# Layer 0: each pair of value products as four products of 32 columns, in a kernel of four graph layers

## What is computed

```
h = relu(layernorm(x))
Q, K, V = h @ Qw + Qb, h @ Kw + Kb, h @ Vw + Vb
S1 = einsum('id,kdh->ikh', Q, A1);  S2 = einsum('jd,kdh->jkh', K, A2)
e = S1[rows[:, None], kidx] + S2[rows[None, :], kidx]       # kidx: the edge's kind, from adj
attn = softmax(leaky_relu(e), axis=1)
x = x + einsum('ijh,jhd->ihd', attn, Vh).reshape(n, h * d) @ Pw + Pb
```

## Time and profile before

| | |
|---|---|
| median of 3 runs | 1069.88 us (1066.89 to 1075.04) |
| the profiled execution, its own time | 1069.17 us |
| its span, first to last instruction | 1066.9 us |
| busy: PE, DVE, POOL, ACT | 941.1, 732.8, 554.4, 552.6 us |
| mean granted clock of TensorE | 0.893 |
| layer 0's loop over tiles | about 94 to 575 us of the span |

### The profile page before, as it was taken

How to read it: one execution, slowest core, us unless ns; L and a number is a source line. 1 busy time by engine, 2 the same in 40 slices (tenths; PEclk the granted TensorE clock), 3 DMA queues, 4 the chain that set the end, 5 groups by cost and what they waited for, 6 DMA issues and landing times.

```text
span 1066.9 us, 14476 instructions
## 1 busy us (share of the span) xinstructions
PE 941.1 (88%) x5214; PEld 331.4 (31%) x5214; DVE 732.8 (69%) x1181; ACT 552.6 (52%) x957; POOL 554.4 (52%) x658
## 2 busy tenths in 40 slices
PE   1998999999999999999999379899968949999970
PEld 1853222222222222222224322233332324555430
DVE  3234777777787777877774558611539577999987
ACT  0465666666566665666652047300120138899970
POOL 2005788888989888898781000000000007899962
PEclk8655999999999999999998569999968965999995
DMA  9472011121112112021000000000000000000000
GB/s 197 75 157 73 11 22 63 34 70 35 66 27 67 37 27 74 22 73 33 22 16 7 0 1 1 1 1 1 1 0 1 1 1 0 1 1 1 0 1 20
DMA packets 24764, 32.99 MB, mean 31 GB/s; under 512 B 16187, under 2 KB 16315, under 8 KB 23670
## 3 DMA queue, kind: packets, MB, share of 16 engines
q1 hardware_dynamic: 22390, 23.69, 7.8%
q0 software_dynamic: 2304, 8.39, 4.3%
HBM read 39.17 MB, written 1.29 MB: 38 GB/s over the span
## 4 chain that ended last, share of the span: by engine, by line
PE 74%; DVE 15%; issue 4%; ACT 3%; DMA 2%; POOL 1%; SPq 1%; DVEq 0%; POOLq 0%
PE ps L1102 22%; PE ps L1112 11%; PE ps L1239 8%; PE ps L1089 5%; DVE big L405 4%; PE ps L1081 4%; PE ps L1187 3%; PE ps L1264 3%; PE ps L1300 3%; PE ps L1032 2%; PE ps L993 2%; DVE big L734 2%; DMA big<-in_L_gnn_Pw_dram 2%; DVE big L402 2%; PE ps L1177 2%
## 5 line engine op out<-in xcount | busy, mean ns | idle before, releaser
L538 DVE COPY_PREDICATED big<-mask,ps 128x512 f32<-128x512 uint8 x512 | 338.4, 723 | 109.4 <-PE ps L1089 102.2
L362 POOL TENSOR_SCALAR big<-big 128x512 f32<-128x512 f32 x512 | 355.2, 710 | 67.2 <-PE ps L1112 66.7
L861 ACT ACTIVATE ps<-ps 128x512 f32<-128x512 f32 x512 | 266.8, 583 | 159.8 <-PE ps L1081 159.8
L1102 PE MATMUL ps<-big 128*64 128x512 f32 x1024 | 258.9, 613 | 0.0
L374 POOL TENSOR_TENSOR big<-big 128x512 f32<-128x512 f32 x40 | 67.3, 1682 | 328.7 <-ACT big L939 328.7
L1112 PE MATMUL ps<-big 128*32 128x512 f32 x1024 | 136.3, 604 | 0.0
L1081 PE MATMUL ps<-op_r,op_l 18*128 18x512 bf16 x512 | 109.7, 385 | 1.8 <-DVE mask L530 1.2
L1102 PEld LDWEIGHTS ps<-big 128*64 128x64 f32 x1024 | 58.6, 136 | 135.6 <-issue 98.7
L1300 PE MATMUL ps<-big 66*128 66x512 f32 x160 | 86.1, 667 | 2.2 <-DVE big L707 1.3
L405 DVE TENSOR_TENSOR big<-big,mask 128x512 f32<-128x512 f32 (+1 forms) x72 | 65.8, 933 | 14.8 <-ACT big L881 13.4
L1089 PE MATMUL ps<-op_r,op_l 9*128 9x512 bf16 x512 | 70.6, 389 | 2.0 <-ACT ps L861 2.0
(11 more groups left out here) (242 smaller groups left out, 1139.7 us busy)
## 6 DMA issues: line engine op xcount, KB each, us to landing
big<-in_adj_dram POOLq DMA_DIRECT2D x16, 512.0 KB, 7.7
big<-max_scratch SPq DMA_DIRECT2D x8, 1024.0 KB, 4.9
big<-rden_scratch SPq DMA_DIRECT2D x30, 256.0 KB, 3.3
op_l<-split_scratch SPq DMA_DIRECT2D x64, 36.0 KB
op_r<-split_scratch SPq DMA_DIRECT2D x64, 36.0 KB
x_nat<-in_x_dram SPq DMA_DIRECT2D x1, 512.0 KB, 4.2
out_dram<-x_nat SPq DMA_DIRECT2D x1, 512.0 KB, 3.8
den_scratch<-y_nat SPq DMA_DIRECT2D x30, 8.0 KB
```

Of the source, the lines that this page charges most:

```text
L362: pool.tensor_scalar(ring[:, k % RING, :], vrow[:, head % 2, i0:i0 + HALF], HUGE, g0[:, head, jt:jt + 1], ALU.min, ALU.max).then_inc(s["ba ...
L538: dve.copy_predicated(ring[:, k % RING, :], mask[:, jt, i0:i0 + HALF], ps[:, k % SLOTS, :])\
L861: act.activation(ps[:, k % SLOTS, :], ps[:, k % SLOTS, :], ACT.Relu, scale=-1.0).then_inc(s["relus"], 1)
L1102: m = pe.matmul(ps[w * D:(w + 1) * D, MAIN, :], vp[:, head, jt + w, :], ring[:, (u + w) % RING, :], start=(jt == 0), stop=(jt == NT - 2))
```

## The change

In `aggregate`, the product of a row tile with its 64 value columns becomes two products with 32 columns each, over the same slot of `ring`. The four products of a call go to the four quarters of bank 6: quarters 0 and 1 are the two halves of tile u's values, quarters 2 and 3 those of tile u + 1. The same numbers come to lie at the same places of PSUM as before. The waits at the head of the call and the semaphore behind its last product stay.

```diff
-                for w in range(2):
-                    m = pe.matmul(ps[w * D:(w + 1) * D, MAIN, :], vp[:, head, jt + w, :], ring[:, (u + w) % RING, :],
-                                  start=(jt == 0), stop=(jt == NT - 2))
+                for w in range(4):
+                    m = pe.matmul(ps[32 * w:32 * (w + 1), MAIN, :], vp[:, head, jt + w // 2, 32 * (w % 2):32 * (w % 2 + 1)],
+                                  ring[:, (u + w // 2) % RING, :], start=(jt == 0), stop=(jt == NT - 2))
                 m.then_inc(s["products"], 1)
```

## The result

The changed kernel takes 1050.66 us, median of 6 runs (1046.70 to 1058.02), against 1068.39 us for the kernel before in the same rounds (1063.26 to 1075.10). The ratio is 0.9868, 95% interval 0.9831 to 0.9905: faster by 1.3%, 17.7 us by the medians. The forecast was 1052.5 us in 1046.5 to 1060.

What follows compares the result with a forecast made beforehand. PE was taken to bound the loop. From the profiled 1069.17 us, 19.8 us saved at width boundaries and 3.0 us lost to DVE gave 1052.4, forecast as 1052.5 us, range 1046.5 to 1060.

Steps and rivals of the forecast that it cites:

- The bound: In layer 0's loop PE is busy 466.93 of 467.60 us, so time spared there comes off the end.
- Streaming and weight loads at no cost: In `aggregate`, four narrow products side by side still take 0.86 us per call and their loads stay hidden: cost 0.
- The boundaries: Between neighbouring product groups in the loop, fewer or cheaper width changes save 12.9 + 5.8 + 1.1 = 19.8 us of PE time.
- denominators followed by values: At 43 such turns in the loop the denominators go from 0.99 or 1.00 to 0.86 us: 5.8 us saved.
- The loss to DVE: Where `cross` already waits for DVE, 27 times, three of four visits lose 0.15 us: 3.0 us, between 0 and 5.3.
- The time: Whole kernel: 1069.17 - 19.8 + 3.0 = 1052.4 us for the profiled execution, forecast as 1052.5 us.
- the clock rival: Behind the loop, low-clock stretches fall otherwise when everything starts earlier: 1046 or 1059 us, chance 0.11.
- The waits: In the loop, POOL's and ACT's waits get smaller by about 17 us.
- DVE as the bound: In the loop, DVE's block work eats more of the gain and L1081's waits double: 1058 to 1062 us, chance 0.12.
- The price not hanging on width: The 0.15 us per group belongs to a semaphore wait or PSUM bank change and stays: 1068 us, chance 0.04.
- A price for each instruction: Added matmul and load pairs in the loop cost time, deciding from 19 ns each; 1075 us at 25 ns, chance 0.03.

Runs made afterwards that it cites:

- mixed kernels: Kernel before with only the second, or only the first, value call of every three units cut to 32-column products: loop 479.5 or 484.7 us, against 480.5 before.

## Why the prediction was right

**The bound.** PE's spared time came off the loop. It stayed the bound: 460.20 of 464.65 us busy.

**Streaming and weight loads at no cost.** Right. A narrow value call takes 0.86 us, and even at twice the instructions it stays there. That rested on the rows of layer 2, where the changed shape already ran in the kernel before.

**The boundaries.** Forecast 19.8 us; the groups gave 19.4 and some tenths. The two mixed kernels show that the cause is the change of width, not the bank, the line or the wait. The term for denominators followed by values was slightly small: 0.135 us for each, and 0.151 measured. That the saving sits in the first call of a group was the chain's way of cutting; by the starts most of it sits at the turn itself (0.100 or 0.114 us) and the rest behind the first passes of the groups. The sum doesn't depend on it.

**The loss to DVE.** The mechanism was right, the size too small: 3.0 forecast, in 0 to 5.3, and 4.4 measured from the 25th `cross` on, 3.4 of them by the additions. The step took `cross`'s 27 waits and let three in four of them lose a visit's gain. What it missed is that there are also new waits, 32 in place of 27 and 11 in place of 3 on the matmul itself, where DVE had just been in time, and that the additions would meet POOL's instructions more often and take 0.99 us instead of 0.71.

**The time.** The loop was forecast 16.8 us shorter and was 15.9 shorter, 15.1 where the clock is the same. The medians differ by 17.7. The 1.8 us more are no part of the mechanism: the stretches ahead of and behind the loop moved by +3.5 and -6.3 us between the two traces, and the executions of one kernel spread over 11 us. So that the measured 1050.66 us lies as near to the forecast as it does is in part luck. Behind the loop it was the clock rival's part: 18 us less at the lower level in the changed trace, and the traces of this unchanged stretch range over 6.6 us. The forecast also took the sum for the profiled execution, 1052.4 us, nearly as it was; carried over to the median by the 0.7 us that it names, it would have been 1053.1.

**The waits.** ACT's and POOL's were to shrink by about 17 us and shrank by 12.8 and 14.5, so here the forecast was too high.

**The rivals.** DVE as the bound: the waits of L1081's weight loads grew by a third and didn't double. The price not hanging on width: out by the mixed kernels. A price for each instruction: at most 1.2 ns where 19 were needed.

## What to carry to other kernels

Where PE sets the end, look at the distance between starts of neighbouring product groups, and compare a group alone with two in a row: what the first costs more is the price of changing the column width, here 0.14 to 0.15 us each time. Cutting the wide products to the narrow width removed it without a cost, with the same number of columns side by side. The gain must be counted in changes of width, not in products: making half of the calls narrow made this loop 4 us longer. After such a gain look at the engine with the irregular extra work: here its 26 long instructions decided how much of it arrived. And compare stretches at the same granted clock, since half a microsecond of a loop can be where the clock rose.

## What the runs showed of the hardware that I had not expected

- A DVE addition of two f32 SBUF tiles (128 x 512), 0.65 us at its shortest, took 4.40 to 4.43 us beside a row of POOL instructions and ended 0.55 us after the row did. One select earlier in the same visit it took 1.87 us at most. Before the change, none of 26 took over 1.21 us.
- A POOL instruction of 0.69 us (L362) took 1.12 to 1.17 us behind such an addition, in 25 of 26 cases before the change; behind an addition of 8 columns it took no more than 0.70.
- Each of five gaps of 1.84 or 1.85 us in PE's matmuls was followed by a fall of the granted clock to 0.50; gaps of 0.84 to 0.90 us weren't. Behind one of them the same eight records took 1.93 instead of 1.04 us.
- At a granted clock of 1.00, 443.4 us of the same loop agreed within 0.02 us in three executions.
- Cutting f32 products from 512 to 256 columns of moving data added at most 1.2 ns for each added pair of matmul and load.
